# Score slots of group g+2 at the end of weighing group g, and halves made ahead of score slots

## The reference

```
h   = wkv(x, fside, fside, w1, u1, cond)             # two-sided decayed sums along the positions, per channel
qkv = h @ w_qkv.T ; 16 heads of 32 channels, causal mask
x   = x + softmax(q k^T / sqrt(32)) v @ w_o.T
r   = wkv(x, fside, fside, w2, u2, cond)
a   = mx(r, 6-bit) ; g = a @ mx(w_gate).T ; u = a @ mx(w_up).T
x   = x + mx(silu(g) * u, 6-bit) @ mx(w_down).T      # mx: blocks of 32 share a power-of-two scale

wkv: ek = exp(min(k,30)), num/den = forward scan + backward scan of ek*v / ek, own term exp(min(u+k,30)),
     result sigmoid(r) * num / max(den, 1e-8) * gain
```

## Time and profile before

| what | us |
|---|---|
| median of 3 runs | 1158.38 (1157.96 to 1158.63) |
| profiled execution | 1161.8 |
| its span, first to last instruction | 1160.0 |
| mean granted TensorE clock | 0.859 |
| PE / DVE / ACT busy | 773.8 / 843.8 / 419.7 |

### The profile page before, as it was taken

One profiled execution on the slowest core, in us unless ns is written; L12 is line 12 of the kernel. 1 busy time (PEld: TensorE's weight loads), 2 busy tenths in 40 slices (PEclk: granted clock), 3 DMA queues, 4 the chain that ended last, 5 costly groups with the idle time before them and its releaser, 6 DMA issues.

```text
span 1160.0 us, 10102 instructions
## 1 busy us (share of the span) xinstructions
PE 773.8 (67%) x3617; PEld 387.2 (33%) x3664; DVE 843.8 (73%) x1160; ACT 419.7 (36%) x698; POOL 27.8 (2%) x31
## 2 busy tenths in 40 slices
PE   0000016546768998977689988876899888878475
PEld 0000002223434443444344434443444344444132
DVE  5999999967668589667786896666868965331567
ACT  3101101315546344156453432554534324333140
POOL 0000000000010000000100000100000000000000
PEclk9999998858677999977779999777799997787797
DMA  8312120034330000543300015433000153320001
GB/s 332 139 45 78 40 81 0 18 78 122 83 82 19 10 1 12 129 141 82 82 19 10 1 30 136 121 77 82 19 9 1 34 127 91 74 48 1 1 0 37
DMA packets 34402, 72.24 MB, mean 62 GB/s; under 512 B 5808, under 2 KB 5808, under 8 KB 32560
## 3 DMA queue, kind: packets, MB, share of 16 engines
q1 hardware_dynamic: 30032, 63.73, 20.1%
q10 hardware_dynamic: 4320, 7.87, 2.0%
HBM read 33.82 MB, written 4.19 MB: 33 GB/s over the span
## 4 chain that ended last, share of the span: by engine, by line
PE 45%; DVE 28%; issue 8%; ACT 8%; SPq 5%; DMA 4%; POOL 0%; ACTq 0%; DVEq 0%
PE bank L1089 6%; PE bank L1166 5%; SPq L295 5%; PE bank L1145 5%; PE bank L1041 5%; PE bank L1105 4%; PE bank L1177 4%; PE bank L1065 4%; PE bank L1034 4%; PE bank L1090 3%; DMA stacks<-halves 3%; DVE region L676 2%; DVE attn L878 2%; ACT region L458 2%; PE bank L1091 2%
## 5 line engine op out<-in xcount | busy, mean ns | idle before, releaser
L851 DVE TENSOR_REDUCE negmax<-bank 128x4 f32<-128x512 f32 (+2 forms) x96 | 99.9, 1041 | 144.0 <-PE bank L1067 143.7
L1034 PE MATMUL bank<-wqkv,h 128*128 128x512 f32 x128 | 61.1, 633 | 179.8 <-DVE h L788 170.9
L1089 PE MATMUL bank<-stacks 128*128 128x512 f32 (+3 forms) x256 | 140.1, 548 | 41.9 <-ACT region L458 23.8
L458 ACT ACTIVATE region<-bank 128x512 f32<-128x512 f32 (+3 forms) x256 | 106.7, 436 | 145.2 <-PE bank L1091 144.1
L1065 PE MATMUL bank<-stacks 128*128 128x128 f32 (+3 forms) x256 | 98.9, 462 | 74.3 <-DMA stacks<-halves 69.3
L1041 PE MATMUL bank<-h,wqkv 128*128 128x512 f32 x256 | 116.0, 602 | 4.8 <-DVE region L997 4.8
L1089 PEld LDWEIGHTS bank<-stacks 128*128 128x128 f32 x256 | 68.4, 267 | 91.2 <-ACT region L458 55.3
L1065 PEld LDWEIGHTS bank<-stacks 128*128 128x128 f32 x256 | 63.7, 251 | 99.0 <-issue 82.7
L1034 PEld LDWEIGHTS bank<-wqkv,h 128*128 128x128 f32 x128 | 25.6, 203 | 212.1 <-issue 202.4
L1090 PE MATMUL bank<-maxrow,pick 128*128 128x384 bf16 (+3 forms) x228 | 95.9, 420 | 0.0
L1177 PE MATMUL bank<-region,down_q 128*128 128x512 bf16 x249 | 62.4, 405 | 26.5 <-DVE region L656 25.8
(11 more groups left out here) (125 smaller groups left out, 1330.1 us busy)
## 6 DMA issues: line engine op xcount, KB each, us to landing
stacks<-halves SPq DMA_DIRECT2D x256, 128.0 KB, 2.5
kt<-in_fside ACTq DMA_DIRECT2D x30, 256.0 KB, 3.1
h<-in_x SPq DMA_DIRECT2D x4, 1024.0 KB, 7.3
region<-in_w_gate SPq DMA_DIRECT2D x4, 1024.0 KB, 12.0
xt<-in_x SPq DMA_DIRECT2D x4, 1024.0 KB, 6.1
region<-in_w_up SPq DMA_DIRECT2D x4, 1024.0 KB, 5.6
region<-in_w_down SPq DMA_DIRECT2D x4, 1024.0 KB, 4.7
out<-xt SPq DMA_DIRECT2D x16, 256.0 KB, 2.9
```

Of the source, the lines that this page charges most:

```text
L458: nc.scalar.activation(probs[:, i, P_AT[t]:P_AT[t] + CAUSAL[t]], bank[4 + n % 2][:, 0:CAUSAL[t]], ACT.Exp, scale=SCALE).then_inc(p_ready, 1)
L851: nc.vector.tensor_reduce(o, scored, AX_X, ALU.max, negate=True).then_inc(max_taken, 1)
L1034: mm = nc.tensor.matmul(bank[4 + t % 2][:, :], h[:, j, P * t:P * t + P], wqkv[:, j, 2 * C:3 * C], start=(j == 0), stop=(j == CJ - 1))
L1089: nc.tensor.matmul(o, ks[s][:, i, P * t:P * t + P], qs[s][:, i, P * t:T], start=True, stop=False)
```

## The change

On PE the slots of group g+1 move one step earlier: slots 0 and 1 of group g+2 stand behind the weighing of group g (those of group 1 behind the first `transpose_maxima`), slots 2 to 5 behind the four heads' units, and none within the weighing. `transpose_maxima(b, g + 1)` moves to the middle of the weighing. Slot 1 gets a wait of its own for `mt_copied`, since `transpose_maxima` writes the bank that slot 1 writes. `project_qk(b + 1, 3, 0)` moves ahead of the down product. On ACT `high_parts(b, 2)` moves ahead of the 16 exponentials of group 0 and `high_parts(b, 3)` into those of group 1; `copy_maxima` comes before `sum_reciprocal`. DVE's order is shifted to fit. In the prelude the last weight is rounded in the order 2, 3, 0, 1, and SP waits for ten chunks where it waited for all twelve.

```diff
 SP     sp.wait_ge(setup, SETUP_STEPS)
-            sp.wait_ge(quartered, 2 * WC + FC)
+            sp.wait_ge(quartered, 2 * WC + 2)
             stack(0, 0)
...
 ACT turn
                 copy_maxima(b, 0)
                 weigh(b, 3, 1)
+                high_parts(b, 2)
+
                 exps(b, 0, 0, 6)
...
                 exps(b, 0, 10, 16)
-                high_parts(b, 2)
                 weigh(b, 4, 0)
...
                     table(6)
+                copy_maxima(b, 1)
+                cap_exp(b, 5)
                 sum_reciprocal(b, 0)
-                copy_maxima(b, 1)
-                exps(b, 1, 0, 6)
-                cap_exp(b, 5)
-                exps(b, 1, 6, 10)
+                exps(b, 1, 0, 4)
                 load_k(b, 4)
                 reciprocals(b, 4)
                 own_exp(b, 5)
-                exps(b, 1, 10, 16)
+                exps(b, 1, 4, 10)
+                high_parts(b, 3)
+                exps(b, 1, 10, 12)
                 weigh(b, 5, 0)
                 weigh(b, 5, 1)
-                high_parts(b, 3)
+                exps(b, 1, 12, 16)
                 cap_exp(b, 6)
-                sum_reciprocal(b, 1)
-
                 copy_maxima(b, 2)
-                exps(b, 2, 0, 4)
                 load_k(b, 5)
                 reciprocals(b, 5)
                 own_exp(b, 6)
-                exps(b, 2, 4, 8)
+                sum_reciprocal(b, 1)
+
+                exps(b, 2, 0, 4)
                 weigh(b, 6, 0)
                 weigh(b, 6, 1)
-                exps(b, 2, 8, 14)
+                exps(b, 2, 4, 12)
                 cap_exp(b, 7)
-                exps(b, 2, 14, 16)
+                exps(b, 2, 12, 16)
...
+                weigh(b, 7, 0)
+                copy_maxima(b, 3)
                 sum_reciprocal(b, 2)
-                weigh(b, 7, 0)
-
-                copy_maxima(b, 3)
...
 ACT, feed-forward steps f
+                    if f == 4:
+                        load_k(b, 9)
                     if f == 5:
-                        load_k(b, 9)
+                        weigh(b, 10, 0)
                     if f == 6:
-                        weigh(b, 10, 0)
-                    if f == 7:
                         weigh(b, 10, 1)
...
 DVE prelude
-            for c in range(FC):
-                u = 8 + c // 2
-                if c % 2 == 0:
+            for k, c in enumerate(ROUNDING):
+                u = 8 + k // 2
+                if k % 2 == 0:
...
 DVE turn
                 forward(b, 3, 1)
+                maxima(b, 1, 0)
                 finish(b, 2)
                 cap(b, 4)
-                maxima(b, 1, 0)
+                maxima(b, 1, 1)
                 backward(b, 3, 0)
                 backward(b, 3, 1)
-                maxima(b, 1, 1)
+                maxima(b, 1, 2)
                 add_own(b, 3)
-                maxima(b, 1, 2)
+                maxima(b, 1, 3)
                 forward(b, 4, 0)
-                maxima(b, 1, 3)
+                maxima(b, 1, 4)
                 forward(b, 4, 1)
-                maxima(b, 1, 4)
-                finish(b, 3)
                 maxima(b, 1, 5)
                 split_maxima(b, 1)
+                finish(b, 3)
...
-                normalise(b, 0)
                 maxima(b, 2, 0)
                 add_own(b, 4)
                 maxima(b, 2, 1)
+                normalise(b, 0)
...
+                maxima(b, 3, 0)
                 normalise(b, 1)
-                maxima(b, 3, 0)
+                maxima(b, 3, 1)
                 finish(b, 5)
-                maxima(b, 3, 1)
...
+                finish(b, 8)
                 for f in range(FJ // 2):
...
-                    if f == 0:
-                        finish(b, 8)
-                    elif f < 3:
-                        backward(b, 9, f - 1)
-                    elif f == 3:
+                    if f < 2:
+                        backward(b, 9, f)
+                    elif f == 2:
                         add_own(b, 9)
-                    elif f < 6:
-                        forward(b, 10, f - 4)
-                    elif f == 6:
+                    elif f < 5:
+                        forward(b, 10, f - 3)
+                    elif f == 5:
                         cap(b, 11)
...
 PE scores(b, g, k)
+                if k == 1 and g:
+                    pe.wait_ge(mt_copied, b * GROUPS + g)
...
 PE turn
                 transpose_maxima(b, 0)
+                scores(b, 1, 0)
+                scores(b, 1, 1)
                 for g in range(GROUPS):
                     nxt = g + 1 < GROUPS
                     for n in range(UNITS):
                         scores_by_key(b, g, n)
                         if n % TT == TT - 1 and nxt:
-                            scores(b, g + 1, n // TT)
-                    weigh_values(b, g, 0, 1)
-                    if nxt:
-                        scores(b, g + 1, 4)
-                    weigh_values(b, g, 1, 2)
-                    if nxt:
-                        scores(b, g + 1, 5)
-                    weigh_values(b, g, 2, TT)
+                            scores(b, g + 1, n // TT + 2)
+                    weigh_values(b, g, 0, 2)
                     if nxt:
                         transpose_maxima(b, g + 1)
+                    weigh_values(b, g, 2, TT)
+                    if g + 2 < GROUPS:
+                        scores(b, g + 2, 0)
+                        scores(b, g + 2, 1)
...
                         project_qk(b + 1, 1, s)
+                    project_qk(b + 1, 3, 0)
                 for n, c in enumerate(ROUNDING):
...
-                    if n < 2 and more:
-                        project_qk(b + 1, 3, n)
+                    if n == 0 and more:
+                        project_qk(b + 1, 3, 1)
```

More of the change, by code:

```diff
@@ L532, in turn @@
                 own_exp(b, 7)
-                sum_reciprocal(b, 2)
                 weigh(b, 7, 0)
                 copy_maxima(b, 3)
+                sum_reciprocal(b, 2)
                 weigh(b, 7, 1)
```

## The result

The changed kernel takes 1087.95 us (median of 4 runs, 1084.52 to 1091.37) against 1158.51 for the kernel before: ratio 0.939, 95% interval 0.936 to 0.942. A second measurement, taken beside its variants, gave 1085.36 and 0.934 (0.931 to 0.938). The forecast was 1097 in a range of 1072 to 1132. The profiled span fell from 1160.0 to 1085.5.

A forecast was written before the change was run, and what follows sets the result against it. Attention was taken as held by a chain passing between engines. Attention 66.1 - 15 - 18 - 3 + 9 = 39, with 8 and 13.8, makes 61 us off 1161.8: 1101, or 1097 as median; range 1072 to 1132.

The forecast's parts named there:

- Parts 1 and 2: Prelude's new rounding order, 8 us off; feed-forward end, projection ahead of the down product, 13.8 us off in all.
- Part 3: Attention: waits for copies, and before groups 1 to 3 for split maxima and maxrow, go; 66.1 us off.
- Part 4a: Attention: slots (1,0) and (1,1), now ahead of group 0's keys, wait for group 1's copies; 15 us added.
- Part 4b: Attention: waiting stays before slot (3,0), 5.5 us in turns 0 to 2, 1.5 in turn 3; sum 18 us.
- Part 4c: Attention: ACT's exponentials of group 1 are cut up in one more place; 3 us added over the kernel.
- Part 5: Attention's clock: two heads and a slot run at full clock as waits between groups 0 and 1 go; 9 us off.
- rival 2: Attention: group 3's copies also come in time and the clock stays up; 24 us more than forecast, 1073; chance 0.13.
- Rival 4: PE falls to 1.2 GHz for the whole of attention, ending at about 1183; chance 0.06 with others slower.
- Rival 1: Attention's waits only move, maxima and maxrow as late as before, clock unchanged; 1132; chance 0.15 together with another rival.

The follow-up runs named there:

- Experiment 7: Changed kernel with transpose_maxima put back to the end of the weighing; 1085.1 us, ratio 0.935.
- experiment 5: Kernel before with only the two high_parts calls moved earlier on ACT, PE and DVE orders kept; 1126.7 us, ratio 0.968.
- Experiment 4: Changed kernel with 14, 14 and 30 added throwaway matmuls in three long PE waits a turn; 1082.2 us, ratio 0.932.
- experiment 8: Changed kernel with slots 0 and 1 of group g+1 put back behind the first head of group g; 1101.5 us, ratio 0.949.
- experiment 10: Kernel of experiment 9 with slots 0 and 1 of groups 2 and 3 put back behind the first head of the group before; 1080.4 us, ratio 0.929.
- experiment 9: Changed kernel with high_parts of group 3 ahead of all exponentials of group 1; 1052.9 us, ratio 0.907.
- experiment 11: Kernel of experiment 9 with leave_low(b, 1) ahead of project_qk(b, 2, 0) on PE; 1044.7 us, ratio 0.901.
- experiment 6: Changed kernel with both high_parts put back behind the exponentials of groups 0 and 1; 1148.9 us, ratio 0.991.
- Experiment 3: Kernel before with added throwaway matmuls in PE's attention waits, no wait taken away; 1138.2 us, ratio 0.980.

## Why the prediction was right, and where its sum was not

- **Parts 1 and 2** were right in place and size: 8 and 13.8 us forecast; 4 to 9 and 16 to 22 measured alone. By the profile of the changed kernel PE goes on 8 us earlier behind the first two slots (244.05 for 252.17), and each turn's rest is 4.5 to 4.7 us shorter.
- **Part 3** named the right waits, but not their worth. The copies of group 2 do come in time: before slot (2,0) PE waits only 0.57 us, in turn 3, where the four turns had 10.6. The waits before slot (3,0) did not go: 28.8 before, 30.0 now. The waits before the later transposes fell from 10.8 to 2.9 (18.4 less 4 x 3.87), at three places beyond the one a turn that the prediction allowed, and those for `maxrow` fell from 17.6 to 0.7. Experiment 7 shows that the transposes' place gave nothing of it.
- **Part 4a** was right as a number (16.6 us measured; my 15 and the 1.1 that stood there before make 16.1) and mostly wrong as to its cause (experiment 5).
- **Part 4b** was the mis-sized term among the waits: 30.0 us for 18 (7.32, 7.18, 7.49 and 8.03). From POOL's start to the slot it was 16.5 us in turn 1, near the 17.6 that I used. But from POOL's start to the end of the weighing (520.19) only 9.3 us passed, not 11 to 12. My sum had reckoned six key units and up to two slots there. By the timeline PE, which runs ahead of ACT's exponentials, had four units (2.5 us), one slot (0.8) and the weighing (5.7) left. In turn 3 I had taken 1.5 and it was 8.03: from POOL's start (934.14) to the end of the weighing (942.06) only 7.9 us passed, and the slot came 16.0 us after POOL's start, nearly as in turn 1. For the 1.5 the sum had no working but the shorter wait before the change.
- **Part 4c** was 3 and came out at 12 (waits for exponentials, 23.8 to 35.9). The prediction had named exponentials that hold PE "for much more than before" as a sign of being wrong, and half as much again is near that. It had called them "short of nothing else", but they stand behind `high_parts(b, 2)`, which waits for copies.
- **Part 5**, the clock, was 9. With the measured terms the ledger of waits leaves 7 us (64.3 gone; 15.5, 30.0 and 12.1 come) where 30 were forecast. PE's busy time carried the other 41.5. So the forecast of 39 for attention, against 49.4 measured, was made of two errors of opposite sign, and that the total came within 10 us of the measured time is in part luck.
- **The ledger itself** is the step to give up. It treats each wait of PE as a cost to be summed. Experiment 4 fills 38 us of waits for copies with work, raises the clock, and gains nothing; experiment 8 takes 42 us of them away and loses 16; experiment 10 leaves them alone and loses 27; experiment 9 takes 30 away and gains 32. In experiment 8 the waits for exponentials took back 22 of the 42, and PE's busy time in the attentions rose by 27.5 us at a clock of 0.76 to 0.84: a ledger that holds one kind of wait fixed misses both. What goes down with the time in most of these kernels is how long DVE waits for slots: 143.7 (before), 85.6 (changed), 55.2 (9), 86.6 (10), 39.5 (11). That is a correlation and in good part arithmetic, since DVE's work in attention is 330 to 339 us in all of them. It has an exception: experiment 6 has 142.9, as before, and attentions 13.9 us longer. That the place of the slots of groups 2 and 3 costs time is shown by experiment 10, on the kernel of experiment 9.
- **The rule** on the clock is that of the Trainium skill, "TensorE: Matmul & The Clock Gate", section "HAM oscillation — how this bites in real kernels": work that stands behind a wait for a transfer starts at the low clock. The trace agrees. The slot behind the wait of 4.58 us runs its 128-column matmuls in 0.45 us where those at 453.50 take 0.30 us. Experiment 3 shows the price of the low clock in the kernel before (23 us), experiment 4 that the changed kernel pays nearly none.
- **The rivals.** The clock did stay higher, as rival 2 had it, but group 3's copies did not come in time (30.0 us of waits). Rival 4 did not happen. Rival 1's thought that waits only move was right for the exponentials.

The parts interact. Outside attention the change gives 25 us. In attention the early halves alone give 32 to 43, the slots and transposes alone lose about 14, and both together gain 45 by the first measurement and 51 by the second. Early halves make it safe to stand slots at the head of the line: without them PE waits 104.6 us for copies there (experiment 6), with them 47.2. That the slots of group 1 also cover ACT's wait for the copies is argued and not shown, since no run moves them alone.

## What to carry to other kernels

When no engine is full, don't add up the waits of one engine. Ask which chain passes through all of them, and look at where the engines with the most fixed work in the stage wait (here DVE, for PE's slots). How long such an engine idles in all follows from the length of the stage and tells nothing more; the place of its waits tells which piece of work comes late. Here two slots made in advance for each of two groups were worth 27 us (experiment 10), while 38 us of filled waits on PE were worth nothing (experiment 4). Two edits that each look like a trade can be worth far more together, so try them in pairs. When a consumer is moved up, move its whole supply chain up with it: one more step moved on ACT (experiment 9) and one on PE (experiment 11) gave another 41 us.

## What the runs showed of the hardware

Matmuls whose result is thrown away, put in TensorE's waits, made the kernel before 23 us faster (ratio 0.980, 0.977 to 0.983): the granted clock over the attentions rose from 0.74-0.79 to 0.83-0.92. The same in the changed kernel raised it from 0.81-0.86 to 0.90-0.97 and gave nothing that can be measured.
